# Eight-core transformer megakernel: the sixteen attention heads of a chunk issued in pairs, on fixed PSUM banks

## The reference

```python
def local_attention(q, k, v):            # b, 16 heads, n = 2048, d = 64
    w = WINDOW                           # 256
    ...
    mask = (it < jb) | (it > jb + w) | (jb == -1)
    sim = jnp.einsum('bhwie,bhwje->bhwij', bq, bk2) * QK_SCALE
    sim = jnp.where(mask, -jnp.finfo(sim.dtype).max, sim)
    attn = jax.nn.softmax(sim, -1)
    out = jnp.einsum('bhwij,bhwje->bhwie', attn, bv2)
...
for i in range(DEPTH):                   # 6
    x = attn_layer(shift_tokens(x), Wqkv[i], q_scale[i], k_scale[i], Wo[i]) + x
    x = ffn_layer(shift_tokens(x), ln_g[i], ln_b[i], W1[i], b1[i], W2[i], b2[i]) + x
```

## Time and profile before

| | us |
|---|---|
| median of 2 timed runs | 34545.68 (34542.23 to 34549.12) |
| profiled execution, its own time | 34582.78 |
| its span on the slowest core (core 1) | 34581.1 |
| spans of the other seven cores | 34207.8 to 34544.8 |
| PE matmul busy | 19741.5 (57%) |
| DVE busy | 9638.7 (28%) |
| ACT busy | 9304.3 (27%) |
| POOL busy | 4348.1 (13%) |

### The profile page before, as it was taken

One profiled execution on the slowest core, in us unless ns is written; L12 is line 12 of the kernel. 1 busy time (PEld: TensorE's weight loads), 2 busy tenths in 40 slices (PEclk: granted clock), 3 DMA queues, 4 the chain that ended last, 5 costly groups with the idle time before them and its releaser, 6 DMA issues.

```text
span 34581.1 us, 303527 instructions; the slowest of 8 cores (34207.8 to 34581.1 us)
## 1 busy us (share of the span) xinstructions
PE 19741.5 (57%) x86528; PEld 8477.3 (25%) x86528; DVE 9638.7 (28%) x21121; ACT 9304.3 (27%) x33416; POOL 4348.1 (13%) x4789
## 2 busy tenths in 40 slices
PE   5544743754755645547438547546456465386867
PEld 2222221221221222222212212212222222122323
DVE  4333133132142241231331321422412313312222
ACT  1134043052151250340430421512503403301111
POOL 0011011011111111111120110111111111100000
PEclk6655765766766656657657657567566576577878
DMA  0110210301302202202103013012022021030101
GB/s 20 30 41 24 58 38 27 79 14 28 77 15 48 56 18 47 56 22 56 49 27 74 19 27 78 15 37 70 14 50 56 21 48 51 27 67 18 20 27 30
DMA packets 938504, 1364.73 MB, mean 39 GB/s; under 512 B 590068, under 2 KB 604264, under 8 KB 936864
## 3 DMA queue, kind: packets, MB, share of 16 engines
q0 software_dynamic: 730752, 668.31, 10.1%
q10 hardware_dynamic: 154752, 570.49, 5.0%
q1 hardware_dynamic: 51360, 106.52, 0.9%
HBM read 1325.55 MB, written 335.54 MB: 48 GB/s over the span
## 4 chain that ended last, share of the span: by engine, by line
PE 48%; ACT 17%; DMA 16%; issue 8%; POOL 5%; DVE 5%; another core or an unknown queue 0%; ACTq 0%; DVEq 0%; POOLq 0%; SPq 0%
PE pb L260 18%; PE pb L1289 8%; DMA xs_t<-xstB 7%; PE pb L1305 7%; PE pb L1359 6%; ACT p_sb L1076 5%; PE pb L1122 4%; ACT pt_sb L1113 4%; DMA w1c<-w 3%; ACT dumpA L956 3%; POOL qkvg L993 2%; ACT qkvg L1002 2%; DMA xstB<-xs 2%; DMA reps<-qs 1%; PE pb L1297 1%
## 5 line engine op out<-in xcount | busy, mean ns | idle before, releaser
L1289 PE MATMUL pb<-xn_fm,w1c 128*128 128x512 bf16 (+1 forms) x8448 | 2653.7, 471 | 1364.8 <-DMA w1c<-w 1364.8
L1122 PE MATMUL pb<-pt_sb,vr 128*64 128x128 bf16 x8640 | 1468.5, 303 | 2217.1 <-ACT pt_sb L1113 2217.1
L1318 ACT ACTIVATE gg<-pb 128x512 f32<-128x512 f32 (+1 forms) x1056 | 630.3, 597 | 7542.4 <-PE pb L1313 7454.6
L1020 PE MATMUL pbt<-ident_bf,qkvg 128*128 128x128 bf16 x3072 | 388.4, 306 | 3671.7 <-POOL qkvg L993 1967.7
L1324 DVE TENSOR_TENSOR prod<-pb,gg 128x512 bf16<-128x512 f32 (+1 forms) x1056 | 729.8, 691 | 6282.1 <-ACT gg L1318 4996.3
L1245 PE MATMUL pb<-ident_sb,xs_t 128*128 128x128 f32 x1536 | 372.6, 424 | 3577.9 <-POOL xs_t L1237 3577.9
L1359 PE MATMUL pb<-w2h,prod 128*128 128x512 bf16 (+1 forms) x8448 | 2339.4, 432 | 76.7 <-DVE prod L1324 40.4
L1305 PE MATMUL pb<-xn_fm,w1c 128*128 128x512 bf16 (+1 forms) x8448 | 2324.6, 425 | 0.0
L1067 DVE SCALAR_TENSOR_TENSOR p_sb<-pb,rstd,lmask 128x384 f32<-128x384 f32 (+2 forms) x3072 | 1816.1, 591 | 1146.2 <-PE pb L1048 1130.1
L260 PE MATMUL pb<-wqkv,xs_fm 128*128 128x512 bf16 x9216 | 2060.3, 385 | 22.5 <-issue 21.3
L1103 PE MATMUL pb<-diag,p_sb 128*128 128x128 bf16 x8640 | 1465.8, 303 | 830.0 <-DVE diag L1094 820.8
(11 more groups left out here) (181 smaller groups left out, 26688.6 us busy)
## 6 DMA issues: line engine op xcount, KB each, us to landing
xstB<-xs ACTq DMA_DIRECT2D x576, 512.0 KB, 3.3
xs<-xstB POOLq DMA_DIRECT2D x352, 512.0 KB, 2.9
xstage<-xs ACTq DMA_DIRECT2D x320, 512.0 KB, 3.2
w1c<-w POOLq DMA_DIRECT2D x504, 256.0 KB, 4.9
xs<-xstage POOLq DMA_DIRECT2D x192, 512.0 KB, 3.0
wqkv<-wqkv POOLq DMA_DIRECT2D x12, 6144.0 KB, 42.6
xs_t<-xstB SPq DMA_DIRECT2D x192, 254.0 KB
w2h<-w POOLq DMA_DIRECT2D x12, 2816.0 KB, 18.9
```

Of the source, the lines that this page charges most:

```text
L1122: return E.matmul(obank[0:64, 0:128], vr[:, (kc % 4) * 1024 + h * 64: (kc % 4) * 1024 + h * 64 + 64], pt_sb[:, pox + j * 128: pox + j * 12 ...
L1289: return E.matmul(abank[0:rows, 0:512], w1c[:, fi * rows: fi * rows + rows] if rows != 128 else w1c[:, fi * 128: fi * 128 + 128], xn_fm[:, ...
```

## The change

The head loop of `emit_chunk` runs over pairs of heads, in ten steps instead of eighteen, and inside a step the parts stand in another order: first both `stage2a` of the pair whose scores were issued one step earlier, then both `stage1` of the next pair, then both `stage2b` of the pair of two steps ago. The banks of S, T and O are no longer taken in turn: S uses pb0 and pb1 (by the head's parity), T pb2 and pb3, O pb4 and pb5. No instruction of computation is added or removed.

```diff
         def stage1(h):
             fc, r0 = h // 2, (h % 2) * 64
-            sbank, sfree = ctx.bank()
+            sbank = ctx.pb[h % 2]
+            sfree = ctx.pb_ev.get(id(sbank))
...
-            tbank, tfree = ctx.bank()
+            tbank = ctx.pb[2 + h % 2]
+            tfree = ctx.pb_ev.get(id(tbank))
...
-            obank, ofree = ctx.bank()
+            obank = ctx.pb[4 + h % 2]
+            ofree = ctx.pb_ev.get(id(obank))
...
-        for h in range(NHEAD + 2):
-            if h < NHEAD:
-                stage1(h)
-            if 1 <= h <= NHEAD:
-                stage2a(h - 1)
-            if h >= 2:
-                stage2b(h - 2)
+        for hp in range(NHEAD // 2 + 2):
+            if 1 <= hp <= NHEAD // 2:
+                stage2a(2 * hp - 2)
+                stage2a(2 * hp - 1)
+            if hp < NHEAD // 2:
+                stage1(2 * hp)
+                stage1(2 * hp + 1)
+            if hp >= 2:
+                stage2b(2 * hp - 4)
+                stage2b(2 * hp - 3)
```

## The result

| | before | after |
|---|---|---|
| median of the timed runs (13 and 14) | 34525.41 us | 34821.79 us |
| ratio, with its 95% interval | | 1.0093 [1.0050, 1.0137] |
| forecast | | 34780 us, +0.7% |

The changed kernel is 0.9% slower, which is under the 2% that one comparison surely tells from no change, yet the interval leaves out 1. The medians are over all timed executions, the ratio over those in which no die (cores 0 to 3, or 4 to 7) ran behind the other at a lower clock; the profiled execution of after, 35059.34 us, is one in which a die did, so its total is not set against that of before.

The account below looks back on a forecast made before the run. PE's and ACT's ways round a head were level at 2.09 us, no engine full. +1.37 per chunk over 168 (+230) and short chunks (+5) gave +235 on 34582.8, 34818; timed median 37.1 lower: 34,780, range 34,520 to 34,990.

Parts of the forecast that it names:

- Second head 1.64, first head 2.71: O-to-O distances in a changed pair: second head 1.64 us, first 2.71; sum 4.35 against 4.17 before, +0.18.
- Chunk 38.32 after, 36.95 before: Heads of a three-key-block chunk, first S to last O: 38.32 us against 36.95, +1.37, over 168 chunks.
- DVE's lead of 1.58 us: Mid-chunk, DVE allows T at 4.06 us, PE reaches it at 5.64; 1.58 slack makes S's bank waits cost nothing.
- Start 7.30: At a chunk's start, first O comes 7.3 us after first S instead of 6.01, behind DVE's work: +1.30.
- Short chunks 5 us: The 24 chunks with one or two key blocks lose 0 to 33 us together; 5 taken.
- Pt waits for T eight or nine times per chunk instead of once: Sign in the heads: pt waits for T once in a pair, some 0.1 to 0.2 us visible before it.
- Everything behind the heads moves one for one: The output projection waits for the last head's oc, so the heads' gain or loss goes on the path one for one.
- a move of more than a few tenths per chunk outside the heads: Sign against the forecast: something outside the heads moves by more than a few tenths per chunk.
- The side look at TensorE's clock: In the heads the granted clock stays 0.50, the 1.2 GHz level; no rise is due.
- 1 (the heads cover each other's waits): ACT copies pt of one head during the other's O, saving 980 us: 33,570 us; chance 3%.
- Rival 2: No change that counts in the heads: a chunk costs 0 to +0.6 us, 34,550 to 34,650; chance 17%.
- rival 4: Denser bursts raise the clock in the heads to 2.4 GHz, some 640 us less, 33,910; chance 2%.

Follow-up runs that it names:

- S late: Changed kernel with both S of a step moved behind its second halves (stage2a, stage2b, stage1); 37685 us beside 34572 for before.
- shifted start: Changed kernel with single heads up to O of head 0, then pairs (1,2), (3,4) and so on, head 15 alone; ratio 1.0006.
- order alone: Kernel before with the new head loop in pairs, banks still taken in turn; ratio 1.0066.
- banks alone: Kernel before, old order of single heads, with only the fixed banks for S, T and O; ratio 1.0011.
- interleaved version: Changed kernel with a pair's second halves interleaved (PE: S, S, T, T, O, O; ACT: exp, exp, pt, pt, oc, oc); ratio 0.9479, then 0.957.
- swapped order: Changed kernel with a pair's second halves swapped: T, pt, O, oc of the odd head first; 37.50 us per median chunk, 34504.80 to 34999.86 us.
- T first: Changed kernel, on PE only, with T of a pair's second head moved ahead of O of its first; ratio 0.9919.
- O and oc put off: Single heads, no pairs, fixed banks, with O and oc put off by one head, against the kernel before; ratio 0.9558.

## Why the prediction was right

- *Second head 1.64, first head 2.71.* Measured 1.65 and 2.68. T put ahead of O took 0.28 out of the second head's distance and left the first head's (2.68) and the start (7.27) as they were, so the cause is shown and not only argued.
- *Chunk 38.32 after, 36.95 before.* 38.22 in the median chunk, 38.28 as a mean; before 36.99. The step was +1.37 and measured +1.29.
- *DVE's lead of 1.58 us hides the new waits of S.* In after T never waits for DVE in mid-chunk, and S waits for a bank only at the start. With the lead taken away by S late, the pair grew to 6.91.
- *Start 7.30.* Measured 7.28. But my wording there, +1.30 as if it were a price, was loose, though the sum was sound: the two more exp in it are saved later. Only 0.27 of it is a loss beside the shifted start, which is delayed a little too.
- *Banks cost nothing.* Shown, 1.0011.
- *Short chunks 5 us.* 9 measured, all of it with two key blocks (+0.86 each); one block loses nothing (-0.09). Too small to matter.
- *About an eighth of the chain is the head loop.* Too low: the listed lines leave out the smaller ones, and from first S to last O the heads take 6925 of 34581 us, a fifth. No term rested on it.
- *Pt waits for T eight or nine times per chunk instead of once.* Nine in a chunk with three key blocks, and head 0's besides, which was there before.
- *Everything behind the heads moves one for one.* Here a term was missing: the gap from the last O to the next chunk's first S grows by some 0.4 us where a projection of q, k and v lies in it, some 70 us in all, as the order alone shows beside the banks alone. The prediction named a move of more than a few tenths per chunk outside the heads as a sign against itself, and this stands at that edge. The side look at TensorE's clock asked only whether it rises in the heads; it does not, but it rises later in the output projection behind them, whose matmuls took a mean of 524 ns before and 553 after. My range took this in, my sum did not.
- *+235 us, 34,780.* The heads gave 226 and the missing term some 70. The measured step, +0.93%, is 320 us with an interval of 170 to 470, so that both sums lie inside it, and that the forecast came within 42 us of the measured median is in part luck.

Of the rivals, 1 (the heads cover each other's waits) did not hold for this change, for the reason given, and held when the order was changed for it. Rival 2 was out (the heads lost 1.29 in each chunk with three key blocks), rival 4 too: a window of after's heads still shows 0.50.

```profile
7590.00:7600.00 10.00, 5.54 (x42) 3.08 (x42) 7.43 (x22) 5.90 (x18) 0.00 (x0) 0.50 0.00 0
```

The Trainium skill's advice to issue matmuls back to back in batches (Perfetto Trace Analysis, Matmul Optimizations) was followed by the change and by the interleaved version alike; one lost 0.9% and the other gained about 5%, and the clock in the heads stayed 0.50 in both. In the projection behind them it rose later with the change (5.49 us behind the last O with the order alone, 4.74 without it) and earlier with the interleaved version (4.37). The advice was not what decided; what decided was what stands ahead of a waiting instruction.

## What to carry to other kernels

Where engines run fixed lists, follow one round of the loop on each engine and write down which handover ends last. What helped here was to put another head's work, on each engine, between the instruction that feeds a wait and the one that waits; interleaved pairs do that, and so do single heads with O and oc put off by one. Pairs with a head's T, pt, O and oc still in a row opened what had been hidden. A wait that grows on an engine that is not the bound is no loss, and an instruction that vanishes under others may come up in the chain when its neighbour is moved.

## What the runs showed that I had not expected

- Behind an oc that writes partitions 64 to 127, ACT's next exp starts 0.28 us later, behind one that writes 0 to 63, 0.16. The swapped order shortened the distance between pairs from 2.68 to 2.57 and the chunk from 38.2 to 37.5, which changed only which of the two stands ahead of the exps. It is not the bank that is read (the order alone). What in the engine makes it, no run here shows.
- The order of the small matmuls in the heads changes the time of the large ones behind them, which are the same in all versions. The granted clock leaves 0.50 inside the output projection, sooner or later by version, and the projection's last matmul moves with it (us behind the chunk's last O, means of all chunks and cores):

| version | clock leaves 0.50 | last matmul starts |
|---|---|---|
| T first | 4.12 | 5.67 |
| both halves interleaved | 4.37 | 5.82 |
| S late | 4.48 | 5.90 |
| before | 4.70 | 6.02 |
| banks alone | 4.74 | 5.98 |
| swapped | 4.75 | 6.03 |
| shifted pairs | 4.82 | 6.07 |
| O and oc put off | 4.84 | 6.06 |
| after | 5.35 | 6.32 |
| order alone | 5.49 | 6.35 |

- The feed-forward matmuls, which no version touches, took 425 ns before (L1305) and 436 after (L1311): over 8448 of them 93 us. The order alone, with the same order of heads as after, has 390. That difference between executions is a third of this change's effect, and why the chunk, not the total, was the measure.
